# Post-norm layer pair on one core: order of the second norm, first feed-forward unit in token parts, last token tile in column halves

## What is computed

```
x = layernorm(x + scan_block(x))             # layer 0: selective scan, 16 states
x = layernorm(x + ffn0(x))                   # silu(x Wg) * (x Wu), then Wd; inner width 1792, fp16 weights
x = layernorm(x + attention(x))              # layer 1: 32 heads of 16, causal, rotary
x = layernorm(x + ffn1(x).astype(float16))   # the same form; inner width 1376, 4-bit weights, unpacked here
```

## Time and profile before

| | us |
|---|---|
| median of 3 runs | 879.1 (876.25 to 879.51) |
| profiled execution, its own time | 876.1 |
| its span in the profile | 874.4 |
| TensorE matmul busy | 804.1 (92%) |
| VectorE busy | 642.1 (73%) |
| ScalarE busy | 443.5 (51%) |
| GpSimd busy | 301.8 (35%) |
| mean granted TensorE clock | 0.972 of full speed |

### The profile page before, as it was taken

The page is one execution under the profiler, slowest core; times in us unless marked ns, Lnnn a source line. Parts: engine busy times, 40 slices in busy tenths (PEclk is TensorE's granted clock), DMA queues, the critical chain, the costliest instruction groups (busy, mean ns, idle before and its releaser), DMA issues.

```text
span 874.4 us, 19489 instructions
## 1 busy us (share of the span) xinstructions
PE 804.1 (92%) x8137; PEld 383.5 (44%) x8137; DVE 642.1 (73%) x900; ACT 443.5 (51%) x584; POOL 301.8 (35%) x217
## 2 busy tenths in 40 slices
PE   7669787787999999999989999999989999999997
PEld 2434344444444444455544444444424444444443
DVE  4999999997565333444669999999976677775344
ACT  4976666546654321254427777777786433332100
POOL 0699899991001000155421222121143222221000
PEclk9589999999999999999988999999999999999999
DMA  6900000005230000000000000000132013330001
GB/s 215 365 3 3 3 3 2 3 4 168 97 115 1 1 0 1 1 1 1 1 1 2 2 2 2 2 2 3 37 115 86 1 59 118 123 110 0 13 36 48
DMA packets 20017, 38.25 MB, mean 44 GB/s; under 512 B 5009, under 2 KB 10961, under 8 KB 19938
## 3 DMA queue, kind: packets, MB, share of 16 engines
q1 hardware_dynamic: 19938, 37.10, 12.4%
HBM read 34.87 MB, written 2.16 MB: 42 GB/s over the span
## 4 chain that ended last, share of the span: by engine, by line
PE 76%; DVE 13%; issue 4%; POOL 3%; ACT 2%; DMA 1%; SPq 1%; DVEq 0%; ACTq 0%; POOLq 0%
PE ps L832 13%; PE ps L613 11%; PE ps L590 10%; PE ps L769 8%; DVE arena L1354 7%; PE ps L702 7%; PE ps L867 7%; PE ps L666 6%; PE ps L753 3%; PE ps L706 3%; POOL arena L1205 2%; PE ps L679 2%; PE ps L509 2%; PE ps L465 1%; PE ps L778 1%
## 5 line engine op out<-in xcount | busy, mean ns | idle before, releaser
L1563 DVE TENSOR_REDUCE arena<-ps 128x1 f16<-128x512 f32 (+3 forms) x320 | 181.4, 630 | 6.4 <-PE ps L706 4.1
L1114 ACT ACTIVATE arena<-ps 128x1024 f32<-128x1024 f32 (+2 forms) x160 | 143.4, 940 | 60.6 <-PE ps L753 58.8
L1205 POOL TENSOR_TENSOR arena<-arena 128x1024 f32<-128x1024 f32 x62 | 152.0, 2485 | 9.3 <-DVE arena L1354 8.9
L1354 DVE TENSOR_TENSOR_SCAN arena<-arena,ps 128x1024 f32<-128x1024 f32 x64 | 142.1, 2269 | 2.0 <-PE ps L509 1.7
L832 PE MATMUL ps<-arena 128*128 128x512 f16 x528 | 114.5, 379 | 1.4 <-DVE arena L1671 1.4
L702 PE MATMUL ps<-arena 64*128 64x512 f16 (+3 forms) x384 | 99.6, 339 | 0.7
L1254 POOL TENSOR_SCALAR_AFFINE_SELECT arena<-arena 128x512 f32<-128x512 f32 x64 | 43.4, 685 | 162.4 <-ACT arena L1114 162.3
L613 PE MATMUL ps<-arena 128*128 128x512 f16 x448 | 97.5, 379 | 1.5 <-DVE arena L1494 1.5
L957 ACT ACTIVATE arena<-arena,negA 128x1024 f32<-128x1024 f32 x64 | 72.8, 1146 | 45.4 <-DVE arena L1354 43.2
L509 PE MATMUL ps<-arena 64*128 64x64 f16 x3072 | 60.0, 196 | 35.1 <-DVE arena L1354 31.8
L509 PEld LDWEIGHTS ps<-arena 64*128 64x128 f16 x3072 | 52.2, 98 | 86.3 <-DVE arena L1354 75.0
(11 more groups left out here) (173 smaller groups left out, 973.1 us busy)
## 6 DMA issues: line engine op xcount, KB each, us to landing
arena<-in_w_q_dram SPq DMA_DIRECT2D x11, 768.0 KB, 4.2
arena<-c_rows SPq DMA_DIRECT2D x16, 512.0 KB, 10.7
arena<-in_w_s_dram SPq DMA_DIRECT2D x11, 384.0 KB, 4.9
arena<-in_x_fm_dram SPq DMA_DIRECT2D x8, 256.0 KB, 4.3
out_dram<-arena SPq DMA_DIRECT2D x8, 256.0 KB, 2.0
arena<-in_wg_dram SPq DMA_DIRECT2D x1, 1792.0 KB, 10.2
arena<-in_wu_dram SPq DMA_DIRECT2D x1, 1792.0 KB, 7.3
arena<-in_wd_dram SPq DMA_DIRECT2D x1, 1792.0 KB, 11.3
```

The source lines that it names most:

```text
L1114: nc.scalar.activation(dst, src, ACT.Exp, scale=float(HD) ** -0.5).then_inc(exp_done, 1)
L1205: nc.gpsimd.tensor_tensor(hC[i % 4][:], hst[i % 3][:], c_all[:, n, :], ALU.mult).then_inc(hc_done, 1)
L1354: nc.vector.tensor_tensor_scan(hst[i % 3][:], dA[i % 3][:], banks(2 * (i % 2), 2), 0.0, ALU.mult, ALU.add).then_inc(scan_done, 1)
L1563: nc.vector.reduce_max(maxima_slot(half, k), ps[:, ring_bank(n), 0:len(heads) * w].rearrange("p (a w) -> p a w", a=len(heads)), AX, negate ...
```

## The change

Three places.

- **Second norm.** VectorE takes the statistics of tile t + 1 and the low half of tile t - 2 before the shift of tile t; ScalarE casts the high half of tile t before the root of tile t + 3 and the normalisation of tile t + 2. TensorE does the gate part of unit 0's first half before the transposes of tile 5, and the up part's four chunks of features in two pairs, before and behind the transposes of tile 7.
- **First unit of the first feed-forward.** 256 tokens at a time: the first once the low halves of tiles 0 and 1 are there, the rest once those of tiles 2 and 3 are. 32 matmuls of 256 columns in place of 16 of 512; gate and up are signalled at the end of the second part.
- **Last token tile.** Its down projection is made in two column halves, in banks 1 and 2 (66 matmuls of 256 columns), each with a signal of its own. VectorE finishes tile 6 before it looks at tile 7, then takes the halves one by one, with one aggregate over both halves' statistics. The loop on TensorE is one pass shorter, and tiles 6 and 7 are written out.

```diff
--- before.py
+++ after.py
@@ -287,6 +287,7 @@
             sem("w1_nib"), sem("w1_full"), sem("w1_scaled"), sem("w1_high"), sem("w1_low"))
         gate1_done, up1_done, silu1_done, h1_done, h1h_done, h1l_done = (
             sem("gate1_done"), sem("up1_done"), sem("silu1_done"), sem("h1_done"), sem("h1h_done"), sem("h1l_done"))
+        last_half, st12 = sem("last_half"), small("st12", [P, 12])
         out_stored = [sem("out_stored0"), sem("out_stored1")]
 
 
@@ -567,11 +568,16 @@
                     if turn:
                         turn_tile(t - 2, t % 2, t < 4)
                 if not straight:
-                    with pe.Fori(2, TT // 2) as k:
+                    with pe.Fori(2, TT // 2 if turn else TT // 2 - 1) as k:
                         for u in range(2):
                             produce(2 * k + u, u, False)
                             if turn:
                                 turn_tile(2 * k + u - 2, u, False)
+                    if not turn:
+                        produce(TT - 2, 0, False)
+                        pe.wait_ge(ln_taken, TT * (ln - 1) + TT - 2)
+                        make(TT - 1, 1, 0, D // 2).then_inc(last_half, 1)
+                        make(TT - 1, 2, D // 2, D).then_inc(ln_in, 1)
                 if between is not None:
                     between()
                 if turn:
@@ -600,7 +606,7 @@
 
 
 
-            def gate_up0(n):
+            def gate_up0(n, lo=0, hi=HALF):
 
                 h, m = divmod(n, M0)
                 gate, up = unit_banks(unit0_slot(n))
@@ -610,9 +616,10 @@
                         pe.wait_ge(free, before + 1)
                     for c in range(DC):
                         for part in (xh, xl):
-                            last = nc.tensor.matmul(banks(bank, 1), w[:, c, m * P:(m + 1) * P], part[:, c, h * HALF:(h + 1) * HALF],
+                            last = nc.tensor.matmul(banks(bank, 1)[:, lo:hi], w[:, c, m * P:(m + 1) * P], part[:, c, h * HALF + lo:h * HALF + hi],
                                                     start=(c == 0 and part is xh), stop=(c == DC - 1 and part is xl))
-                    last.then_inc(signal, 1)
+                    if hi == HALF:
+                        last.then_inc(signal, 1)
 
             def turn_first(t):
                 if t >= 4:
@@ -638,8 +645,10 @@
             turn_first(5)
             turn_normed(3)
             pe.wait_ge(ld_w0, 2 * 16)
+            pe.wait_ge(xl_done, TT // 4)
+            gate_up0(0, 0, HALF // 2)
             pe.wait_ge(xl_done, TT // 2)
-            gate_up0(0)
+            gate_up0(0, HALF // 2, HALF)
             turn_first(6)
             turn_normed(4)
             gate_up0(1)
@@ -820,13 +829,13 @@
                     last = nc.tensor.transpose(ps[:, 2 + t % 2, c * P:(c + 1) * P], xn[:, t % 2, c * P:(c + 1) * P], ident_sb[:])
                 last.then_inc(x_turned, 1)
 
-            def gate_up1(m, u, halves=(0, 1), first=False, only=(0, 1)):
+            def gate_up1(m, u, halves=(0, 1), first=False, only=(0, 1), chunks=tuple(range(DC))):
                 for w, bank, free, signal in ((0, 4 - 4 * u, silu1_done, gate1_done), (1, 6 - 4 * u, h1_done, up1_done)):
                     if w not in only:
                         continue
                     if not first:
                         pe.wait_ge(free, m - 1)
-                    for c in range(DC):
+                    for c in chunks:
                         for s, part in ((0, x3h), (0, x3l), (1, x3h)):
                             for h in halves:
                                 last = nc.tensor.matmul(banks(bank + h, 1), gu[u][:, s, w * DC + c, :],
@@ -841,14 +850,15 @@
                 second_turn(t)
                 second_out(t + 4)
             second_turn(4)
-            second_turn(5)
             pe.wait_ge(w1_low, 1)
             pe.wait_ge(xl_done, 2 * TT + TT // 2)
             gate_up1(0, 0, (0,), first=True, only=(0,))
+            second_turn(5)
             second_turn(6)
             pe.wait_ge(ln_taken, TT + 7)
-            gate_up1(0, 0, (0,), first=True, only=(1,))
+            gate_up1(0, 0, (0,), first=True, only=(1,), chunks=(0, 1))
             second_turn(7)
+            gate_up1(0, 0, (0,), first=True, only=(1,), chunks=(2, 3))
             pe.wait_ge(xl_done, 3 * TT)
             gate_up1(0, 0, (1,), first=True)
             for m in range(1, 3):
@@ -859,12 +869,12 @@
                     pe.wait_ge(w1_low, 2 * k + 2 + v)
                     gate_up1(2 * k + 1 + v, 1 - v)
 
-            def down1(t, u):
+            def down1(t, u, lo=0, hi=D):
                 for m in range(M1):
                     if isinstance(t, int) and t == 0 and m == M1 - 1:
                         pe.wait_ge(h1l_done, M1)
                     for part, s in ((h1h, 0), (h1l, 0), (h1h, 1)):
-                        last = nc.tensor.matmul(banks(u, 1), part[:, m, ds(t * P, P)], wd1[:, s, m, :],
+                        last = nc.tensor.matmul(banks(u, 1)[:, lo:hi], part[:, m, ds(t * P, P)], wd1[:, s, m, lo:hi],
                                                 start=(m == 0 and part is h1h and s == 0), stop=(m == M1 - 1 and s == 1))
                 return last
             pe.wait_ge(silu1_done, M1)
@@ -1157,10 +1167,10 @@
             second_root(2)
             second_normalise(1)
             for t in range(TT - 2):
+                second_high(t)
                 if t + 3 < TT:
                     second_root(t + 3)
                 second_normalise(t + 2)
-                second_high(t)
             second_high(TT - 2)
             second_high(TT - 1)
 
@@ -1455,7 +1465,15 @@
                 take(0)
                 own.done(stats(0))
                 variance(0, 0)
-                for t in range(TT):
+                def take_last(src_bank, lo, hi):
+
+                    dve.wait_ge(x_kept, TT * ln)
+                    src = xtok[:, TT - 1, lo:hi]
+                    own.done(nc.vector.tensor_scalar(o_half[:, lo:hi], banks(src_bank, 1)[:, lo:hi], scale, None, ALU.mult))
+                    own.done(nc.vector.tensor_tensor(src, src, o_half[:, lo:hi], ALU.add))
+                    at = 6 * lo // (hi - lo)
+                    own.done(nc.vector.bn_stats(st12[:, at:at + 6], src))
+                for t in range(TT if turn else TT - 2):
 
                     u, more = t % 2, t + 1 < TT
                     if more:
@@ -1471,6 +1489,19 @@
                         low(t - 1, 1 - u)
                     if t + 1 == TT and turn:
                         low(TT - 1, 1)
+                if not turn:
+                    dve.wait_ge(x_normed, TT * ln + TT - 2)
+                    root_taken(TT - 2, 0)
+                    normalise(TT - 2, 0)
+                    dve.wait_ge(last_half, 1)
+                    take_last(1, 0, D // 2)
+                    dve.wait_ge(ln_in, TT * ln + TT)
+                    take_last(2, D // 2, D)
+                    nc.vector.bn_aggr(mv[:, 1, :], st12[:]).then_inc(var_done, 1)
+                    dve.wait_ge(var_done, TT * ln + TT)
+                    dve.wait_ge(x_normed, TT * ln + TT - 1)
+                    root_taken(TT - 1, 1)
+                    normalise(TT - 1, 1)
             XH, XL = {0: xh, 1: xh}, {0: xl, 1: xl}
 
             def first_stats(t):
@@ -1672,12 +1703,15 @@
                                         x3h[:, :, t * P:(t + 1) * P], ALU.subtract).then_inc(xl_done, 1)
             second_stats(0)
             second_stats(1)
-            for t in range(TT):
+            second_shift(0)
+            second_stats(2)
+            second_shift(1)
+            for t in range(2, TT - 1):
+                second_stats(t + 1)
+                second_low(t - 2)
                 second_shift(t)
-                if t + 2 < TT:
-                    second_stats(t + 2)
-                if t >= 2:
-                    second_low(t - 2)
+            second_shift(TT - 1)
+            second_low(TT - 3)
             second_low(TT - 2)
             second_low(TT - 1)
             def ffn1(m, u, first):
```

## The result

The changed kernel takes 873.61 us in the median of 20 runs (871.03 to 876.63), the kernel before 876.15 (873.99 to 879.51, 20 runs). The ratio is 0.9959, with a 95% interval of 0.9947 to 0.9972: 0.4% faster, 3.6 us (2.5 to 4.6). It is not the ratio of the two medians: these differ by 2.5 us (0.29%), at the low end of that interval. The profiled execution took 873.16 us with a span of 871.4.

A forecast was written before the change was run, and what follows sets the result against it. TensorE, busy 92% of the span, was taken to bound the kernel. Gains of 3.33 + 0 + 1.54 = 4.87 us, subtracted from 877.7 (mean of four executions), gave 872.9 us; range 869.4 to 877.2.

The forecast's parts named there:

- Part 1: Second norm's new order: TensorE's holes of 2.11 and 1.40 us shrink to 0.5, gain 3.33 us, bounds 0 and 3.51.
- Part 2: First feed-forward's first unit in two token parts: TensorE's 1.7 us lead returns as 1.5 to 2 us holes, gain 0.
- part 3: Last tile in column halves: passes gain 1.23 us, store 0.4, matmuls cost 0.09; sum 1.54, bounds -5.6 and 1.7.
- The forecast of over 0.5%: Whole kernel: faster by more than 0.5% (4.4 us), given a chance of 0.60.
- turn is late: Second norm: one handover slips 0.6 to 0.8 us at two tight places, gain there 2.1, total 3.6 us; 16%.
- the weights come late: After the second norm: TensorE waits 3.3 us before a later unit, only the last tile's gain remains, 876.2 us; 7%.
- the walk: Second norm's new order stepped through with old durations: the unit's second half starts at 698.64, not 701.97, 3.33 us sooner.
- the store: Kernel's end: the last store, no longer sharing engines with tile 6's, lands in 2.0 us, not 2.4; gain 0.4.
- the narrow matmuls: Last tile: 66 matmuls of 256 columns at 0.109 us each cost 0.09 us more than 33 of 512.
- The slower rival: Last tile: a half-width matmul costs the full one's 0.216 us, kernel 2.2 us slower at 879.9; 3%.
- lower bound of -5.6: Last tile in column halves: lowest gain in us, if half-width matmuls cost as much as full ones.
- Nothing in the trace tells them apart: Old kernel's four executions, at 876.1, 876.25, 879.1 and 879.51 us: the trace shows no difference between the two pairs.

The follow-up runs named there:

- the fourth experiment: Changed kernel with the first norm's tiles 6 and 7 normalised before ScalarE's first SiLU; the fifth unit started 25.4 us behind the first turn, no total given.

## Why the prediction was right, and where its terms were off

The measured 873.6 us lie 0.7 above the 872.9 forecast and well inside the range; the sign was right, and the traces show the mechanism of parts 1 and 2 and of the shorter passes in part 3. That it came so close is partly luck: the base of 877.7, the mean of four executions, was 1.55 above the median of 20 (876.15), and the gain of 4.87 was 0.54 above the 4.33 of the stages. From the measured base the same gain gives 871.3, 2.3 us too low. The two errors pull opposite ways. The forecast of over 0.5% just missed: 0.41% was measured (0.28 to 0.53%).

- **Part 1** (forecast 3.33, measured 3.28): right to 0.05, in size and in each step. Tile 3's low half, the gate matmuls in the first hole, the last low half under the up part: all as walked. The "turn is late" rival did not happen, nor did the weights come late: the stretch behind is 165.98 us with or without it. What the walk didn't have is the clock behind the hole: 1.7 us in two of five profiles, which would make the part worth some 0.7 us more on average than its holes, as an estimate (2/5 of 1.7, from five profiles only, and if the hole is what lets the clock fall).
- **Part 2** (forecast 0, measured 0 within the scatter of its stage): right. The lead is given back at the last transposes (0.41 to 0.59 us) and before the fifth unit (0.98 or 0.99), in each of the five profiles that have the part and TensorE's order of the diff, without the filled holes; together that is the 1.5 to 2 us of holes forecast, or just under it. That ScalarE's chain holds the unit is what the waits name, and the 12.07 us from the first to the third SiLU, with and without the lead, bear it out; the fourth experiment agrees only in so far as a later SiLU made a new hole. What makes that chain as long as it is stays open.
- **Part 3** (forecast 1.54, measured 1.05): the term that failed is the store. "Alone, the last should take 2.0: gain 0.4" took the 2.4 us of the earlier trace rows for the last store, with contention as its cause. Its end stands 2.45 us behind the last normalisation now, with no other store near, and 2.52 before: 0.06, and less than that over all profiles (2.45 to 2.54 in eight, 2.51 to 2.56 in six). Taken one by one, the 2.4 us are the first of the eight stores, tile 0's, in both kernels; those of tiles 6 and 7 landed in 2.0 each before, 0.8 us apart as they were. So there was no contention to take away, as the trace of before could have told. The passes on VectorE were 0.1 us dearer than summed (an aggregate of 12 numbers 0.21 + 0.03, root until reciprocal 0.43 and not 0.38, for this time VectorE really waits for it), and the narrow matmuls 0.14 us, not 0.09. On the rule of at least 512 elements (the Trainium skill, "VectorE: DVE Perf Modes", section on the TRN2 errata): the 256-column passes paid their fixed part (0.42 and not 0.35 us) as it says, and the part that paid it twice was hidden.
- **The sum**: 4.33 by the stages against 4.87. Three comparisons of the changed kernel gave ratios of 0.9959, 0.9928 and 0.9959, or 3.6, 6.3 and 3.6 us; 4.33 is inside the first and third interval and at the edge of the second (0.9904 to 0.9951). The six runs of the second had a mean granted clock of 0.973 against 0.970 of the kernel before, so part of the 6.3 is the clock; whether the norm hole's is among it is not shown.
- **The slower rival** is refuted: (7.12 + 0.14)/66 = 0.110 us per 256-column matmul, far from 0.183. (The lower bound of -5.6 in part 3 counts the 0.09 for narrow matmuls twice: 1.63 less 7.13 is -5.5.)
- **"Nothing in the trace tells them apart"**, of the executions at 876 and 879, was wrong. 16 of the 20 runs lie between 874.0 and 876.9 and four between 878.5 and 879.5, but the 29 runs of the first comparison fill the gap, from 873.7 to 881.7, so there are no two levels. What goes with the time is the mean granted clock (correlation -0.81 in these 29 runs).

## What to carry to other kernels

Price a reordering at the stage, between marks that are released by the same thing in both kernels: there it repeated to 0.02 us at one clock, where totals scatter by 5. In a woven pipeline, take a result out of PSUM before starting the next tile's chain, and give TensorE independent matmuls to do behind each of the last tiles; here the two brought their full gain only together. A lead that one engine gained was worth nothing here, since the chain of the engine that it met next did not move.

## What I had not expected of the hardware

- A hole of 2.11 us in TensorE's work was followed by 1.2 GHz in two of five profiles, at a price of 1.6 to 1.7 us for the next 12 matmuls, nearly as much again as the hole; both of these had been at 1.2 GHz at the stage's start too, the other three had not.
- Dense filling of two holes (1.96 and 1.47 us) did not keep the clock up: it fell at 459.4 and not at 450 to 454, for the same 10.2 us, and there it cost 2 us more. The low stretch there lasted 6.8, 10.2, 13.6 or 17.1 us, and around 100 us, in the scan, it was 0, 3.4 or 6.8 us in total; the first turn came at 203.4 to 203.9 us where that was 0, and at 205.3 to 207.7 where it was not.
- Matmuls of 128 columns with a fresh weight load each took 56 ns, 2.3 above their share of a 512-column one's time (3 ns for each added matmul), with 98 ns in the row of a load.
- A single 256 KB store took as long to the end of the span as one 0.8 us behind another (2.45 and 2.52 us).
